# Feed forward of a gated cross-attention layer: transposes by 32 by 32 blocks on VectorE and through device memory in place of TensorE's

## What is computed

```python
x = x + tanh(g_xattn) * cross_attention(layernorm(x), ctx, mask, bias)
x = x + tanh(g_ffn) * ffn(layernorm(x), c1, c2, w1, w2t)

def ffn(xf, c1, c2, w1, w2t):            # c1 16x512, c2 1792x16, w1 and w2t 1792x512
    inter = xf @ c1.T @ c2.T             # 1792 selector values per token
    idx = argmax(inter in blocks of 32) + arange(0, 1792, 32)   # 56 of 1792, the first of equals
    h = relu(einsum('bkm,bm->bk', w1[idx], xf))
    return einsum('bk,bkm->bm', h, w2t[idx])
```

## Time and profile before

| what | value |
|---|---|
| runs of the kernel | 1850.5 us median of 3 (1849.65 to 1850.67) |
| the profiled execution | 1849.7 us, its span 1847.5 us |
| granted TensorE clock | 1.0 |
| TensorE (PE) busy | 1833.6 us, 99% |
| TensorE weight loads (PEld) | 1580.0 us, 86% |
| VectorE (DVE) busy | 1089.4 us, 59% |
| ScalarE (ACT) busy | 686.3 us, 37% |
| GpSimd (POOL) busy | 955.5 us, 52% |
| DMA | 359.51 MB, mean 195 GB/s |
| TensorE's share of the chain that ended last | 79% |

### The profile page before, as it was taken

One profiled execution on the slowest core, in us unless ns is written; L12 is line 12 of the kernel. 1 busy time (PEld: TensorE's weight loads), 2 busy tenths in 40 slices (PEclk: granted clock), 3 DMA queues, 4 the chain that ended last, 5 costly groups with the idle time before them and its releaser, 6 DMA issues.

```text
span 1847.5 us, 37822 instructions
## 1 busy us (share of the span) xinstructions
PE 1833.6 (99%) x15260; PEld 1580.0 (86%) x15260; DVE 1089.4 (59%) x1774; ACT 686.3 (37%) x1761; POOL 955.5 (52%) x758
## 2 busy tenths in 40 slices
PE   9999999999999999999999999999999999999999
PEld 7899988899998888888878888888888888888887
DVE  5444467433346465333457676786676887777673
ACT  4322233322233233333346556555555422222221
POOL 5767688766668888778735334333333121111110
PEclk9999999999999999999999999999999999999999
DMA  5555566644455554467658878798787650000000
GB/s 183 198 173 185 192 203 201 211 143 161 142 188 189 183 186 165 165 219 244 230 206 359 339 277 319 301 377 347 274 328 292 249 200 25 26 25 23 24 12 18
DMA packets 131293, 359.51 MB, mean 195 GB/s; under 512 B 12080, under 2 KB 53424, under 8 KB 120624
## 3 DMA queue, kind: packets, MB, share of 16 engines
q1 hardware_dynamic: 131120, 357.09, 53.9%
HBM read 229.11 MB, written 127.93 MB: 193 GB/s over the span
## 4 chain that ended last, share of the span: by engine, by line
PE 79%; DVE 2%; DMA 1%; ACT 1%; issue 1%; POOL 0%; DVEq 0%; SPq 0%; ACTq 0%
PE bank L1488 23%; PE bank L1490 22%; PE bank L1489 22%; PE bank L1589 3%; PE bank L1553 3%; PE bank L1569 2%; PE bank L1702 1%; PE bank L1679 1%; DMA x_tile<-in_x 1%; ACT scores L891 0%; PE bank L1658 0%; DMA ln_x<-in_x 0%; DVE attn_sum L1296 0%; DVE attn_t_lo L1268 0%; POOL wv_s_lo L751 0%
## 5 line engine op out<-in xcount | busy, mean ns | idle before, releaser
L1488 PE MATMUL bank<-tokens_hi,wkq_hi 128*128 128x512 f32 x888 | 346.8, 391 | 1.5 <-DVE tokens_lo L1063 0.8
L1489 PE MATMUL bank<-tokens_lo,wkq_hi 128*128 128x512 f32 x888 | 345.7, 389 | 0.0
L1490 PE MATMUL bank<-tokens_hi,wkq_lo 128*128 128x512 f32 x888 | 345.5, 389 | 0.0
L751 POOL TENSOR_TENSOR wkq_lo<-raw_wkq,wkq_hi 128x768 fp32r<-128x768 f32 x126 | 278.6, 2232 | 122.3 <-ACT wkq_hi L856 122.3
L1488 PE MATMUL bank<-wv_s_hi,tokens_hi 128*128 128x256 f32 x896 | 253.8, 283 | 1.5 <-POOL wv_s_lo L751 1.5
L1490 PE MATMUL bank<-wv_s_hi,tokens_lo 128*128 128x256 f32 x896 | 253.6, 283 | 0.0
L1489 PE MATMUL bank<-wv_s_lo,tokens_hi 128*128 128x256 f32 x896 | 253.6, 283 | 0.0
L1488 PE MATMUL bank<-wo_hi,attn_t_hi 128*128 128x512 f32 x512 | 205.7, 402 | 1.2 <-DVE attn_t_lo L1268 1.2
L1488 PEld LDWEIGHTS bank<-tokens_hi,wkq_hi 128*128 128x128 f32 x888 | 166.7, 188 | 39.3 <-DVE c L1113 3.0
L1490 PE MATMUL bank<-wo_hi,attn_t_lo 128*128 128x512 f32 x512 | 199.8, 390 | 0.0
L1489 PE MATMUL bank<-wo_lo,attn_t_hi 128*128 128x512 f32 x512 | 199.3, 389 | 0.0
(11 more groups left out here) (148 smaller groups left out, 3688.4 us busy)
## 6 DMA issues: line engine op xcount, KB each, us to landing
k_t<-c SPq DMA_DIRECT2D x128, 256.0 KB, 2.4
v_by_token<-c SPq DMA_DIRECT2D x128, 256.0 KB, 2.3
q_t<-c SPq DMA_DIRECT2D x128, 256.0 KB, 2.3
kt<-k_t SPq DMA_DIRECT2D x16, 2048.0 KB, 9.7
qt<-q_t SPq DMA_DIRECT2D x16, 2048.0 KB, 14.2
v<-v_by_token SPq DMA_DIRECT2D x16, 2048.0 KB, 12.8
raw_wkq<-in_wk SPq DMA_DIRECT2D x32, 512.0 KB, 4.1
raw_wv<-in_wv SPq DMA_DIRECT2D x16, 1024.0 KB, 5.4
```

The lines of the kernel that those rows point to most:

```text
L751: pool.tensor_tensor(lo, job_raw(r)[:, a:b, :], hi.bitcast(F32), ALU.subtract)\
L1488: pe.matmul(o, a[0], b[0], start=first_mm, stop=False, skip_group_check=not grouped)
L1489: pe.matmul(o, a[0], b[1], start=False, stop=False, skip_group_check=not grouped)
L1490: return pe.matmul(o, a[1], b[0], start=False, stop=last_mm, skip_group_check=not grouped)
```

## The change

The transposes of the feed forward leave TensorE. VectorE's `transpose` turns 32 by 32 blocks in place within each band of 32 partitions: `xn` in one piece of 128x512, `h_picked` in two of 128x1024 and 128x768 (`turn_h`). SP stores the turned tile to device memory (`store_xf`, `store_h`) and reads it back (`load_xf`, `load_h`) so that a block that stood in band q stands where its features are on the partitions: `raw_xft` and `raw_h_t`. The order of features that results differs from the one before, so the host lays `c1`, `w1` and `w2` out in the same order (`by_block`).

ScalarE and VectorE now make the high and low parts of h from `raw_h_t` in SBUF, and GpSimd takes over the low parts of x (`fx_lo`). `c1` holds high and low parts side by side in one 128 wide tile, and `low_rank` on TensorE is 8 matmuls of 256 columns in place of 12.

Every engine's loop is written anew and runs further ahead, iteration `j` from -1 to 16. TensorE: `output(j - 1)` in one piece; for odd `j` `low_rank((j + 3) // 2)`; then `hidden(j + 2, k)` and `selector(j + 3, k)` by turns. The PSUM banks are dealt out again: the inner values go round banks 4, 5, 1, 6, 0, the selectors round 2 and 3, the output has bank 7 only. Norms and turns of the first four tiles move to earlier steps of attention. Eight buffers hold `x_tile` in place of five, the SBUF arena goes from 207 to 222 KB a partition, and the scratch space for DMA descriptors is set to 1024.

```diff
 def ffn_uses():
+    sel, hid = (2, 3), (4, 5, 1, 6, 0)
...
+    for j in range(-1, PAIRS + 1):
+        if j > 0:
+            out.append((("out", j - 1), 7))
+        if j % 2 and j + 3 < PAIRS:
+            out.append(next_of(sel, ("t", (j + 3) // 2)))
         for k in range(4):
...
+                out.append((("h", 1, 1), 7) if (j, k) == (-1, 1) else next_of(hid, ("h", j + 2, k)))
+            if j + 3 < PAIRS:
+                out.append(next_of(sel, ("sel", j + 3, k)))
...
 # SP
+            def store_h(t, i):
+                sp.wait_ge(dve_hb, 2 * t + i + 1)
+                sp.dma_start(h_d[i][t], hmb[i][:, :]).then_inc(h_out[i], 16)
+            def load_h(t, i):
+                sp.wait_ge(h_out[i], 16 * (t + 1))
+                if t:
+                    sp.wait_ge(dve_hl, 4 * (t - 1) + 2 * i + 2)
+                sp.dma_start(hraw[i][:, :, :], h_d[i][t].rearrange("(q g) (r f) -> (g r) q f", q=4, r=4))\
+                    .then_inc(h_in[i], 16)
...
 # GpSimd
+            def fx_lo(t):
+                pool.wait_ge(act_fx, t + 1)
+                pool.tensor_tensor(xft_part(t, 1), by_chunk(xfr[t % 2], 0, CH), xft_part(t, 0).bitcast(F32), ALU.subtract)\
+                    .then_inc(pool_fx, 1)
...
+                if j + 3 < PAIRS:
+                    rank(j + 3)
+                if j % 2 == 0 and j + 4 < PAIRS:
+                    fx_lo(j + 4)
+                    fx_lo(j + 5)
 # VectorE
             def f_norm(ts_):
...
+                    ln_norm(LN + t, fxn[:, :], x2[t % X2R][:, :])
+                    dve.wait_ge(dve_xn, LN + t + 1)
...
+                    dve.transpose(fxb[t % 2][:, :], fxn[:, :]).then_inc(dve_xb, 1)
...
+            def turn_h(t, i):
+                a, w = HALF[i]
+                dve.wait_ge(dve_hm, 4 * t + 2 * i + 2)
+                if t:
+                    dve.wait_ge(h_out[i], 16 * t)
...
+                dve.transpose(hmb[i][:, :], hm[:, a:a + w]).then_inc(dve_hb, 1)
...
+            for j in range(-1, PAIRS + 1):
+                if j % 2 == 0 and j + 4 < PAIRS:
+                    f_norm((j + 4, j + 5))
+                if j + 2 < PAIRS:
+                    block_rank(j + 2)
+                    first_max(j + 2)
+                if 0 <= j < PAIRS:
+                    for g in range(4):
+                        ht_lo(j, g)
+                if j > 0:
+                    finish(j - 1)
+                if j % 2 and j + 3 < PAIRS:
+                    low_rank((j + 3) // 2)
                 for k in range(4):
                     if j + 2 < PAIRS:
+                        pick_h(j + 2, k)
+                        if k % 2:
+                            turn_h(j + 2, k // 2)
+                    if j + 3 < PAIRS:
+                        block_max(j + 3, k)
+                    if k == 2 and j % 2 and j + 5 < PAIRS:
+                        f_stats((j + 5, j + 6))
+                if j + 3 < PAIRS:
+                    mark_max(j + 3)
 # TensorE
-            def f_transpose_x(t):
...
-            def transpose_h(t, k):
...
             def low_rank(u):
...
+                for k, x_part in enumerate(xft[u % 2]):
+                    for c in range(CH):
+                        mm = pe.matmul(bank[f_bank[("t", u)]][:, 0:FU], c1s[:, c, :], x_part[:, c, :],
+                                       start=k == 0 and c == 0, stop=k == 1 and c == CH - 1)
...
+            for j in range(-1, PAIRS + 1):
+                if j > 0:
+                    for k in range(4):
+                        output(j - 1, k)
+                if j % 2 and j + 3 < PAIRS:
+                    low_rank((j + 3) // 2)
                 for k in range(4):
+                    if j + 2 < PAIRS:
+                        hidden(j + 2, k)
+                    if j + 3 < PAIRS:
+                        selector(j + 3, k)
```

More of the change, by code:

```diff
@@ L414, in dest @@
             if kind == "c1":
[L415 removed]
+                return [c1s[:, :, :].rearrange("p a b -> p (a b)")] * 2
             a = i * PIECE
@@ L705, in _ @@
                 load_w2(n)
-            for t in range(PAIRS):
-                sp.wait_ge(dve_o, t + 1)
-                sp.dma_start(out[t], x2[t % X2R][:, :]).then_inc(out_sem[t % X2R], 16)
-                if t + X2R < PAIRS:
-                    load_x2(t + X2R)
+            load_x2(6)
+            load_x2(7)
+            store_h(0, 0)
+            for j in range(-1, PAIRS + 1):
+                ahead = j % 2 == 0 and j + 4 < PAIRS
+                if j + 1 < PAIRS:
+                    store_h(j + 1, 1)
+                if ahead:
+                    store_xf(j + 4)
+                    store_xf(j + 5)
+                if j + 1 < PAIRS:
+                    load_h(j + 1, 0)
+                if ahead:
+                    load_xf(j + 4)
+                    load_xf(j + 5)
+                if X2R <= j + 6 < PAIRS:
+                    load_x2(j + 6)
+                if j + 1 < PAIRS:
+                    load_h(j + 1, 1)
+                if j > 0:
+                    sp.wait_ge(dve_o, j)
+                    sp.dma_start(out[j - 1], x2[(j - 1) % X2R][:, :]).then_inc(out_sem[(j - 1) % X2R], 16)
+                if j + 2 < PAIRS:
+                    store_h(j + 2, 0)
             for k in range(X2R):
@@ L830, in _ @@
                         do_lo(n)
[L831 to L836 removed]
+            for j in range(-1, PAIRS):
+                if j % 2 and j + 5 < PAIRS:
+                    do_rstd(LN + j + 5)
+                    do_rstd(LN + j + 6)
+                if j + 3 < PAIRS:
[3 more added lines that the diff above has]
+                    fx_lo(j + 5)
         @block.scalar
```

327 lines of the change are left out of this document (132 added, 195 removed).

## The result

The changed kernel takes 1869.6 us, median of 4 runs (1869.35 to 1870.73), beside 1850.1 for the kernel before: a ratio of 1.0108, 95% interval 1.0096 to 1.0121, so 19.5 us or 1.1% slower. The forecast was 1861, slower by 0.6%, with a range of 1846 to 1872.

The account below looks back on a forecast made before the run. TensorE's own work was taken as the old bound, a ring through four engines as the new. -37.5 + 6.3 + 1.0 + 7.4 + 8.5 + 22.0 + 3.7 - 0.7 = +10.7 gave 1860.4, with 0.8 for the median 1861 us, range 1846 to 1872.

Parts of the forecast that it names:

- What TensorE loses: Feed forward: transposes of h and x leave TensorE and the low rank shrinks, -37.5 us in all.
- The ring: Steady feed forward: dependency loop through VectorE, GpSimd, TensorE and ScalarE, 45.4 us per two tiles against TensorE's 41.0; +22.0, chance 0.57.
- TensorE waits 6.3: Start of feed forward: TensorE, ready at 1494.0, waits for VectorE's low rank 1 subtraction until 1500.5; +6.3 us.
- The first pairs' earlier norms and turns lie in attention, where VectorE has idle time: Attention: this early work costs nothing; without that cover, four norms held by GpSimd cost up to 2 us each.
- The other waits at the start: TensorE waits 1.0 us for a selector bank, 7.35 before the first output product, 8.5 in iteration 1.
- The store of h: Start of feed forward: tile 0's store, issued behind w2 and two tiles of x, lands near 1508.6.
- The end: Last three outputs share one PSUM bank; the last two each wait 1.85 us for an update, +3.7.
- No holding: Rival: GpSimd does not hold VectorE's second norm and first_max; 10 us less in five pairs, 1851; chance 0.15.
- GpSimd's low parts at 2.0: Rival: low parts of x take 2.0 us, not 1.27, delaying low rank and first_max; 1874; chance 0.13.
- Dear transposes of h on VectorE: Rival: turns of h cost VectorE more, up to 1.40 and 1.05 us; 1863, no separate chance given.
- TensorE stays the bound: Rival: low rank subtraction finishes before the first hidden group, so only start and end cost; 1831; chance 0.15.
- The rule that an SBUF source costs VectorE 62 cycles less than a PSUM source: VectorE's low parts of h would be 0.06 us shorter, the sum 3 us lower; not counted.

Follow-up runs that it names:

- no_rank: Changed kernel with GpSimd's rank (the choice among equal selectors) left out in 55 of 56 blocks: 1841.9 us, ratio 0.9958.
- all_orders_lowrank_later: Changed kernel with VectorE's subtraction and picks reordered, attention norms spread, h stores early, last outputs in separate banks, TensorE's low rank later: 1825.3 us, ratio 0.9863.
- picks_behind: Changed kernel with VectorE's third and fourth pick and second turn of h moved behind is_max, beside GpSimd's rank: 1857.4 us, ratio 1.0042.
- lowrank_first: Changed kernel with VectorE's low rank subtraction right behind first_max, ahead of the low parts of h and the output update: 1866.2 us, ratio 1.0087.
- norms_late: Changed kernel with the two norms and turns of x behind block_first and first_max in even iterations: 1881.5 us, ratio 1.0170.
- h_stores_first: Changed kernel with SP storing tile 0's turned h ahead of the last four w2 pieces and two tiles of x: 1866.8 us, ratio 1.0086.
- xlo_before_rank: Changed kernel with GpSimd's low parts of x ahead of its rank, ScalarE's high parts ahead of its last selector copy: 1883.9 us, ratio 1.0178.

## Why the prediction was right, and where it was not

- **What TensorE loses** was right: 40.9 against 41.0 for two tiles (no_rank, all_orders_lowrank_later). Over eight pairs 45.63 - 40.86 is 38.2, for the 37.5 of the sum.
- **The ring** was right in size, 45.2 to 45.5 against 45.4, and in its parts: the held second norm (2.96), the rank's wait (3.71), first_max (2.24), the turns (1.25 and 0.98). That it bounds, and not VectorE's busy time, is shown by picks_behind (nothing less to do, 12 us gained) and no_rank (TensorE-bound). What it did not say is that a second ring, by GpSimd's low parts of x, lies 1.8 behind the first. lowrank_first, worked out from the first ring alone, missed by 12.
- **"TensorE waits 6.3"** for the selector of tile 2 was right as a duration (6.7) and 7.2 too early as a time (released at 1500.5 by the forecast, at 1507.7 in the trace), and that is the step that failed: "The first pairs' earlier norms and turns lie in attention, where VectorE has idle time". Idle time in the mean of a slice says nothing of a run of 5.4 us between two steps that TensorE needs. The sentence named a cost if that cover is gone, up to 2 us for each of four norms held by GpSimd, and the sum took nothing. Only one of the four was held, by 1.2 (1.74 in place of 0.54); the cost came from the length of the run and from late loads. Of the 7.2 the traces tie 5.2 to waits of TensorE in attention and 0.9 to the variation at 1230.
- **The other waits at the start** were forecast as 1.0, 7.35 and, in iteration 1, 8.5, of which 6.8 before low rank 2. The trace has none, 6.9 and 4.1. TensorE's own work between them was longer than summed, 21.1 and 12.1 where 18.2 and 9.5 were forecast, at a granted clock of 0.62 in the 7.3 us behind the first wait and of 0.80 behind the first output. That took up waiting time and not the span, since VectorE's chain sets when the waits end. The sum of the start held; how it is shared between work and waits was not foreseen.
- **The store of h** was 9 us later than forecast (1517.7 against 1508.6), but 7.1 of that came with the late start of everything. It was rightly named as behind `w2` in SP's list, but its landing was read off the end of the traffic before, where the new stores and the later end of attention were not in it. By h_stores_first it cost 2.3 by the traces, or 4.1 by the times.
- **The end** was right: 1.7 for each of two updates against 1.85, and 88.7 against 87.7 from low rank 7 on.
- **Rivals.** No holding: refuted by norms_late. GpSimd's low parts at 2.0: they take 1.25. Dear transposes of h on VectorE: refuted by 1.25 and 0.98. (The 6 us in that rival is too high on its own figure: 0.31 for each 128 columns makes the turns in the ring 4.1 longer. It entered no term.) TensorE stays the bound: it did not, and its price was some 3 us low. The version that removes the ring's reasons comes to 1825, where 1831, less 5 for a better start, was written, but it also has the end's waits of 3.4 taken away, which the 1831 contained.
- The rule that an SBUF source costs VectorE 62 cycles less than a PSUM source (the Trainium skill, VectorE: DVE Perf Modes, the TRN2 errata) would have made the low parts of h 0.06 us shorter. They are 0.682 from SBUF and 0.689 from PSUM, 0.007 apart; for this form of instruction the measurement speaks against the estimate, and it was right to leave it out of the sum.

## What to carry to other kernels

Taking work off the bounding engine is worth what it frees only if the order elsewhere lets it: here 4.8 us for two tiles were gained on TensorE, and a ring through four engines, 45.4 long by sums from the old trace, gave all of it back until instructions that nobody waits for were moved under the wait and the one that everybody waits for was moved ahead of them. Work out every way round such a ring, not only the longest, since an edit that shortens one leaves the next. And a wait that the profile names is where slack shows, not what causes it: of two edits that each took a named wait away, one gained 3.9 and one lost 13.

## What was not expected of the hardware

- Behind a gap of TensorE the granted clock is at the lower of its two levels, 1.2 in place of 2.4 GHz: in xlo_before_rank, after 4.11 us without work, the matmuls stood 0.43 apart in place of 0.23 for some 5 us (0.50 in the first window there). Not every gap has it: of the three windows of the changed kernel each begins behind a wait of 2.3, and the first two show 0.96 and the third, with a further wait of 1.5, 1.00. What decides between them was not looked into. In the changed kernel this cost nothing visible, since slack behind the gap took it up (42.9 of work and 2.3 of waiting, or 41.35 and 4.2, both 45.2 to 45.5). In lowrank_first, where the ring runs through that stretch, it cost 1.5 for a pair.
- Holding seems to go both ways: GpSimd's low parts of x took 3.79 for two in attention, beside VectorE's work, and 2.50 in the steady part, and its rank 3.83 beside the held norm (at 1526.18) and 3.59 in the odd iteration behind it. No edit tested this.
